# Moving the recurrence's right side and new state from VectorE to TensorE and ScalarE, in a delta-rule attention and mixture-of-experts kernel

## What is computed

```python
def step(S, inp):                                   # over the 2048 tokens
    q_t, k_t, v_t, b_t = inp
    v_new = (v_t - jnp.einsum('bhd,bhdm->bhm', k_t, S)) * b_t[..., None]
    S = S + jnp.einsum('bhd,bhm->bhdm', k_t, v_new)
    o_t = jnp.einsum('bhd,bhdm->bhm', q_t, S)
    return (S, o_t)
...
q = silu(_short_conv(x @ Wq.T, conv_q))             # the same for k and v; q, k normalized per head
...
final = (gathered * topk_w[:, :, None]).sum(1)      # 8 of 32 experts per token
```

## Time and profile before

| | |
|---|---|
| time, median of 3 runs | 3475.85 us (3452.18 to 3496.45) |
| the profiled execution | 3492.34 us, its span 3490.4 us |
| busy share of the span | PE 75%, DVE 62%, ACT 45%, POOL 30% |
| mean granted clock of PE | 0.853 |
| first phase | to about 1757 us |

### The profile page before, as it was taken

How to read it: one execution, slowest core, us unless ns; L and a number is a source line. 1 busy time by engine, 2 the same in 40 slices (tenths; PEclk the granted TensorE clock), 3 DMA queues, 4 the chain that set the end, 5 groups by cost and what they waited for, 6 DMA issues and landing times.

```text
span 3490.4 us, 109752 instructions
## 1 busy us (share of the span) xinstructions
PE 2631.6 (75%) x46188; PEld 1980.0 (57%) x46188; DVE 2150.8 (62%) x4702; ACT 1565.4 (45%) x2625; POOL 1051.2 (30%) x1028
## 2 busy tenths in 40 slices
PE   3568788887877888865389999978988898544354
PEld 2345555555555555554278888866777777322232
DVE  4779988888888988872332222123444444757665
ACT  4455554555555555511134444435545555323232
POOL 0000333233333333333321111044434431556560
PEclk8778888888888888866699999989999999776676
DMA  6000111111113311111189999977888886333331
GB/s 247 14 9 25 61 49 64 54 61 60 61 62 110 101 58 56 44 56 56 58 291 329 342 343 342 322 253 253 283 269 274 270 272 200 101 99 95 94 94 30
DMA packets 240349, 511.79 MB, mean 147 GB/s; under 512 B 38770, under 2 KB 63860, under 8 KB 239732
## 3 DMA queue, kind: packets, MB, share of 16 engines
q1 hardware_dynamic: 133396, 270.32, 23.5%
q0 software_dynamic: 49152, 134.28, 12.3%
q10 hardware_dynamic: 57312, 100.16, 7.9%
HBM read 303.82 MB, written 200.80 MB: 145 GB/s over the span
## 4 chain that ended last, share of the span: by engine, by line
DMA 53%; PE 25%; issue 7%; DVE 6%; ACT 4%; SPq 3%; POOL 0%; ACTq 0%; POOLq 0%; DVEq 0%
DMA scr_xs<-xn_r,idx 37%; DMA yg<-scr_ys,idx_y 15%; PE ps L632 11%; PE ps L640 6%; PE ps L621 3%; DVE tmp L1430 1%; DVE tu L1433 1%; SPq L823 1%; SPq L830 1%; DVE conv L1360 1%; PE ps L709 1%; DMA xt<-scr_xs 1%; PE ps L380 1%; PE ps L672 1%; DMA out<-x 1%
## 5 line engine op out<-in xcount | busy, mean ns | idle before, releaser
L855 POOL DMA_INDIRECT scr_xs<-xn_r,idx x512 | 531.1, 1037 | 1666.6 <-DMA scr_xs<-xn_r,idx 1325.4
L873 POOL DMA_INDIRECT yg<-scr_ys,idx_y x512 | 519.9, 1016 | 695.8 <-DMA yg<-scr_ys,idx_y 486.6
L632 PE MATMUL ps<-xT,wr 128*128 128x256 f32 x2544 | 616.4, 386 | 0.0
L1725 DVE TENSOR_TENSOR h<-sg,ps 128x256 f32<-128x256 f32 x318 | 133.1, 420 | 687.7 <-ACT sg L1110 687.3
L632 PEld LDWEIGHTS ps<-xT,wr 128*128 128x128 f32 x2544 | 469.9, 194 | 61.9 <-issue 8.6
L1752 DVE SCALAR_TENSOR_TENSOR x<-yg,wsel,x 128x256 f32<-128x256 f32 x512 | 248.0, 486 | 228.0 <-DMA yg<-scr_ys,idx_y 209.6
L640 PE MATMUL ps<-wr,h 128*128 128x256 f32 x1272 | 333.3, 385 | 60.3 <-DVE h L1725 34.2
L640 PEld LDWEIGHTS ps<-wr,h 128*128 128x128 f32 x1272 | 242.5, 192 | 100.8 <-DVE h L1725 36.6
L918 ACT ACTIVATE y<-ps 128x512 f32<-128x512 f32 x318 | 189.8, 597 | 204.2 <-PE ps L640 204.2
L1110 ACT ACTIVATE sg<-ps 128x256 f32<-128x256 f32 x318 | 122.0, 384 | 347.1 <-PE ps L632 346.3
L918 ACT ACTIVATE xT<-ps 128x512 f32<-128x512 f32 x382 | 225.4, 594 | 71.5 <-PE ps L621 36.2
(11 more groups left out here) (244 smaller groups left out, 4106.6 us busy)
## 6 DMA issues: line engine op xcount, KB each, us to landing
wr<-in_wexp SPq DMA_DIRECT2D x318, 384.0 KB, 4.9
xt<-scr_xs SPq DMA_DIRECT2D x318, 256.0 KB, 4.6
scr_ys<-y ACTq DMA_DIRECT2D x318, 256.0 KB, 4.5
scr_xs<-zeros SPq DMA_DIRECT2D x128, 256.0 KB, 3.1
x_in<-in_x SPq DMA_DIRECT2D x64, 128.0 KB
x_res<-in_x SPq DMA_DIRECT2D x64, 128.0 KB
scr_xs<-xn_r,idx POOLq DMA_INDIRECT x512, 3.2
scr_x<-x_res SPq DMA_DIRECT2D x16, 512.0 KB, 2.7
```

What stands on the lines that cost most here:

```text
L632: last = pe.matmul(ps[:, bank, half * TILE:(half + 1) * TILE], wr[:, t % NW, at:at + EI], xT2[:, t % NH, k, :], start=k == 0, stop=k == G - 1)
L855: nc.gpsimd.indirect_dma_start(xs[i // HB][:, :], bass.IndirectOffsetOnAxis(idx[:, i % NR, c, k:k + 1], 0), xn_r[:, i % NR, c, :], None).t ...
L873: nc.gpsimd.indirect_dma_start(yg[:, n % NG, k, :], None, ys[h][:, :], bass.IndirectOffsetOnAxis(idx_y[:, i, c, k:k + 1], 0))\
```

## The change

- `right_side` leaves DVE. A new function `from_inputs` on PE puts `bv` into the PSUM accumulator first (four matmuls of 32x32 by 256 columns per chunk, one for each quarter of the partitions, with the identity `eye` as weights), and `from_state` adds onto it. ACT then copies the sum to `r_sb`.
- `new_state` leaves DVE. ACT does it with two copies of 128 columns, each scaled by a column of `par`, which takes the place of the mask.
- DVE's last calls of a round were `solve_back`, `positions`, `products`, `new_inputs`, `shared_rows`, `token_rows`. They are now `solve_back`, `products`, `new_inputs`, `token_rows`, `shared_rows`, `positions`.
- The three lists of the round are laid anew. On PE the recurrence's calls follow each other sooner and `ranks` comes last. On ACT the calls are grouped so that fewer changes of the function table lie between them. The convolution goes in the order q, v, k instead of k, q, v.
- `token_rows` gets one more wait, for `from_state` of two blocks before. The second phase's code is not touched.

```diff
+            def from_inputs(j, c):
+                n = NC * j + c
+                pe.wait_ge(s_bv, j + 1)
+                if n:
+                    pe.wait_ge(s_rev, n)
+                    pe.wait_ge(s_uev, n)
+                for q in range(4):
+                    pe.matmul(ps[quad(q), RU, 0:D].rearrange("p (n m) -> p n m", m=2 * HD), eye[quad(q), :],
+                              bv[quad(q), j % 2, :, :, c, :].rearrange("p g b m -> p (g b) m"),
+                              start=True, stop=False, skip_group_check=True)
...
-                                                 s_sb[quad(q), g, b, :], start=kind == 0 or (g == 0 and b == 0),
-                                                 stop=kind == 0, skip_group_check=kind == 1)
+                                                 s_sb[quad(q), g, b, :], start=kind == 1 and g == 0 and b == 0,
+                                                 stop=kind == 0, skip_group_check=True)
...
-            CONV_ORDER = (2, 3, 0, 1, 4, 5)
+            CONV_ORDER = (0, 1, 4, 5, 2, 3)
...
+            def right_side(j, c):
+                n = NC * j + c
+                act.wait_ge(s_r, n + 1)
+                nc.scalar.activation(r_sb[:], ps[:, RU, 0:D], ACT.Copy).then_inc(s_rev, 1)
+
+            def new_state(j, c):
+                n = NC * j + c
+                act.wait_ge(s_ku, n + 1)
+                act.wait_ge(s_qs, n + 1)
+                for e in range(2):
+                    last = nc.scalar.activation(s_sb[:, :, :, e * HD:(e + 1) * HD].rearrange("p g b m -> p (g b) m"),
+                                                ps[:, ST, 0:D].rearrange("p (n e m) -> p n e m", e=2, m=HD)[:, :, e],
+                                                ACT.Copy, scale=par[:, e:e + 1])
+                last.then_inc(s_sev, 1)
...
-            def right_side(j, c):
-                n = NC * j + c
-                dve.wait_ge(s_r, n + 1)
-                dve.wait_ge(s_bv, j + 1)
...
-            def new_state(j, c):
-                n = NC * j + c
-                dve.wait_ge(s_ku, n + 1)
-                dve.wait_ge(s_qs, n + 1)
...
                 if Bs:
                     solve(26, 31)
+                if Ps:
+                    gated(p, 1)
+                if Bs:
                     solve_back(b_)
-                if Ps:
+                if A:
+                    products(a)
+                    new_inputs(a)
+                    token_rows(a)
+                if Ps:
+                    shared_rows(p)
                     positions(p)
-                if A:
-                    products(a)
```

More of the change, by code:

```diff
@@ L584, in _ @@
                     project(a, 6)
+                if Ps:
+                    logits(p)
                 if C:
                     to_state(j, 2)
+                if Ps:
+                    shared_up(p, "SU", 1, 0)
+                    shared_up(p, "SG", 0, 1)
+                if C:
                     to_output(j, 2)
                 if A:
+                    norms(a, 1)
+                if C:
+                    from_inputs(j, 3)
+                if A:
                     norms(a, 0)
+                    norms(a, 3)
                 if C:
@@ L1032, in _ @@
                     key_halves(b_)
+                if C:
+                    right_side(j, 0)
+                    new_values(j, 0)
                 if Ps:
@@ L1082, in _ @@
                     betas(a, 0)
+                if Ps:
+                    sigmoids(p)
+                if A:
+                    silus(a, 2)
+                    silus(a, 3)
+                if C:
+                    new_state(j, 2)
+                if Ps:
+                    gate(p, 1)
                 if C:
@@ L1092, in _ @@
                 if C:
-                    new_values(j, 3)
-                if A:
-                    raised(a, 2)
-                    norms(a)
-                    silus(a, 5)
-                if C:
+                    right_side(j, 3)
+                if A:
+                    raised(a, 0)
+                    raised(a, 2)
+                    silus(a, 5)
+                    norms(a)
+                if C:
+                    new_values(j, 3)
                     new_rows(j, 3)
+                    new_state(j, 3)
             def tile_in(t):
@@ L1652, in _ @@
                     solve(7, 11)
-                if C:
-                    right_side(j, 1)
-                if Bs:
                     solve(11, 14)
-                if A:
-                    taps(a, 2, 3)
-                if Bs:
-                    solve(14, 16)
-                if C:
-                    new_state(j, 1)
-                if Bs:
-                    solve(16, 19)
-                if Ps:
-                    gated(p, 0)
                 if A:
@@ L1669, in _ @@
                 if Bs:
+                    solve(14, 16)
+                    solve(16, 19)
+                if A:
+                    taps(a, 4, 5)
+                if Bs:
                     solve(19, 22)
-                if C:
-                    right_side(j, 2)
+                if A:
+                    taps(a, 2, 3)
+                if Ps:
+                    gated(p, 0)
                 if Bs:
```

168 lines of the change are left out of this document (70 added, 98 removed).

## The result

| | before | after |
|---|---|---|
| median of 20 runs each, same sessions | 3476.03 us (3452.18 to 3496.45) | 3494.95 us (3472.31 to 3508.68) |
| ratio, 95% interval | | 1.0049 (1.0029 to 1.0069) |
| the profiled execution, its span | 3492.34, 3490.4 us | 3500.18, 3498.4 us |

The change is 0.5% slower. That is far within the 2% of which I spoke, but its interval is clear of 1, and on the other side than the forecast of 3466 us. It lies inside the range of 3425 to 3500 us.

What follows compares the result with a forecast made beforehand. The string of one-at-a-time scatters was taken to bound the first phase; start -2.6, pace -9 and tail +2 us made about -10 us, so 3475.85 became 3466 us, range 3425 to 3500 us.

Steps and rivals of the forecast that it cites:

- The frame: First phase's end: start 326.4 us, plus 13 blocks of scatters (1397.3 us), plus 34.7 us of tail; round length not in it.
- The string: POOL's unbroken run of 512 scatters from `xn_r`, each waiting for the one before; 108.7 us a block against 96.2 a round.
- the crossing: Block from which `route_rows` waits for scatters of three blocks earlier; forecast at p = 9.2, so block 10 instead of 13.
- The start: First scatter, after `positions` of block 0: 5.1 and 6 us gained, 8.5 lost, -2.6 us in all (-7 to +6).
- The tail: Last `route_rows` to first tile load: `choose` 4 us earlier, `positions` behind `shared_down` 6 us later, +2 us (0 to +5).
- The pace: Time per scatter over 416 scatters: more standing time in shorter rounds speeds them, -9 us (0 to 18 gained).
- The rounds: One `route_rows` to the next: 96.2 to about 92 us (88 to 99), from DVE savings and fewer waits, less 1 us on PE.
- The upper bound: PE's sixteen new small matmuls a round priced as full ones of 386 ns: 6.2 us, against the 1.0 taken.
- the second rival: PE becomes the bound, slowed by waits on ACT; decides only from 101.9 us a round; 3515 us at 105; chance 0.06.
- standing rounds: Rounds of blocks 10 to 13, each with some 13 us more standing time, 53 us in all, letting scatters run faster.
- The first: Rival: rounds don't get shorter, as waits for ACT replace those for DVE; 3475 us; chance 0.16.
- The third: Rival: scatters quicken and the rounds' gain comes through; 3349 us, or 3410 at 3.2 us a scatter; chance 0.10.

Runs made afterwards that it cites:

- a_early: Kernel after with `positions` before `products` and `ranks` before `shared_down` again, in all rounds; ratio to the kernel before 1.0010.
- a_early0: Kernel after with `positions` and `ranks` moved forward again only in the round of block 0; ratio to the kernel before 1.0024.
- a_early15: Kernel after with `positions` and `ranks` moved forward again only in the last round, block 15; ratio to the kernel before 1.0031.
- b_late: Kernel before with `positions` moved to the end of DVE's round; ratio to the kernel before 1.0039.
- b_math: Kernel before with the change's arithmetic alone (`from_inputs` on PE, `right_side` and `new_state` on ACT), other calls in the old order; ratio 1.0040.
- b_k1: Kernel before with one of eight scatters left and the second phase's tiles read from a zeroed stretch; ratio to the kernel before 0.9752.
- aeg_f11: Kernel after with `positions` and `ranks` early, second `gated` early, two scatters in flight from block 11; ratio to the kernel before 1.0231, chip 5.
- b_flight2b: Kernel before with two scatters in flight throughout, on chip 10; ratio to the kernel before 0.9816.
- b_f11: Kernel before with two scatters in flight from block 11 on, on chip 7; ratio to the kernel before 0.9831.
- b_f11b: Kernel before with two scatters in flight from block 11 on, on chip 5; ratio to the kernel before 1.0173.
- b_f11c: Kernel before with two scatters in flight from block 11 on, on chip 10; ratio to the kernel before 0.9809.

## Why the prediction was wrong, point by point

**The frame held.** The string is unbroken, its start, its pace and the tail set the end of the first phase, and a round isn't in the sum as long as it stays below the crossing. a_early, a_early0, a_early15 and b_late move start and tail and with them the time; b_math makes the rounds 5 us longer and they still don't enter the sum; b_k1 gives the 1645 us that the rounds reach alone. This is so on chips like 7 and 10; on 5 and 9 rounds and string are near a tie.

The forecast failed in the terms. The start was to gain 11.1 us against a cost of 8.5, and gained 3.4 against a cost of 11.1. The tail was to gain 4 us from an earlier `choose`, which was no earlier, and its detour cost 7.4 instead of 6. The pace was to give 9 us from shorter rounds, which got longer, and gave 1.6.

**The start: +7.8 us instead of -2.6, outside of its bounds (-7 to +6).** The cost was right as far as it went (8.5 us for the calls that `positions` was moved behind), but a wait that the move makes was missing, and the gain was too large. The timeline of DVE of the kernel after, in round 1:

```profile
317.83 1.18 DVE L1426 SCALAR_TENSOR_TENSOR nq<-conv,sq 128x1024 f32<-128x1024 f32 x1
...
327.54 1.28 DVE L1609 TENSOR_TENSOR x_res<-x_res,ps 128x512 f32<-128x512 f32 x2 [2.61 <-PE ps L512]
```

`products` starts at 317.83 us. Before, `positions` stood at the same place in the list, behind `solve_back`. It started at 321.18 us:

```profile
321.18 0.25 DVE L1552 TENSOR_TENSOR posv<-ps,ecap 128x128 f32<-128x128 f32 x1
```

So rounds -2 to 1 gained 3.4 us, not the 11.1 that I had added up (5.1 for the removed operations and 6 for the waits behind them). The operations are gone, but DVE came to its next wait for PE sooner by as much: `products` of round 0 did start 7.3 us earlier (224.2 against 231.5 us), and in round 1 the waits of `pair_tiles` for PE (5.69, 1.01 and 3.81 us before the first three) gave most of it back. Behind `products` DVE waits 2.61 us for `shared_down`, a call that `positions` had not stood behind. Then 8.5 + 2.6 - 3.4 = 7.7, near the 7.8 of the scatter.

And even the 3.4 us are within the spread. The three kernels with the new arithmetic and `positions` in its early place (a_early, a_early0, aeg_f11) start the string at 321.3, 325.9 and 327.6 us, and the ten with the old arithmetic and the early place at 320.9 to 327.4.

**The tail: +7.4 us instead of +2 (bounds 0 and +5).** The timeline of DVE in the last round of the kernel after:

```profile
1752.62 0.68 DVE L1602 TENSOR_TENSOR h_s<-sq_o,ps 128x512 f32<-128x512 f32 x1
1760.24 1.29 DVE L1609 TENSOR_TENSOR x_res<-x_res,ps 128x512 f32<-128x512 f32 x2 [6.94 <-PE ps L512]
```

I had `choose` 4 us earlier for its new place between the two `gated`. It ends 23.5 us after `route_rows` in both kernels. Then the second `gated`, behind it, lets `shared_down` start only then, and DVE, with nothing else to do, waits 6.94 us for it before `positions`. The sixteen records of `shared_down` take 6.73 us here against 4.60 before; the granted clock over them is 0.54, near the lower of its two levels (1.2 GHz), and was 0.78. PE had stood idle for 4.68 us before them. Before the change `shared_down` ran beside `positions`, and nothing in the tail waited for it. I had counted 6 us for the detour and a gain that did not exist.

**The rounds: 98.1 us instead of 92 (bounds 88 to 99).** Two sizes were off. DVE's own saving was 2.45 us a round, near the 2.7 to 3.3. PE's cost was not 1.0 us. The groups by line of PE in ten rounds of the kernel after (count, busy us, mean ns):

```profile
L392 PE MATMUL ps<-bv,eye 32*32 32x256 f32 x320 | 31.8, 460 | 1.4 <-issue 1.4
```

That is 3.2 us a round. I had the price of a column from the earlier trace rows, where "128 small matmuls" stand in 1.99 us. The trace has two records for each float32 matmul: these 16 matmuls a round show as 32 records, and so the 128 records of the earlier trace rows were 64 matmuls. By that the same sum gives 2.0 us; the rest of the miss is that wide 32x32 matmuls run less densely than the narrow ones. The upper bound was halved in the same way: the 2544 records of the earlier trace rows are 4 matmuls for each of 318 tiles, so that a full matmul has two records of 386 ns and sixteen make 12.4 us. With that in place of 6.2, a round could have passed the 101.9 us of the second rival, and its condition was not as far away as I wrote. And the waits moved instead of ending: 4.2 us a round that stood on `r_sb` and `s_sb` no longer do (1.3 more stand as "issue" before `solved`), those for `h_s` rose from 2.6 to 4.9 us. PE's account of a round is 78.8 busy, 9.0 issue, 8.3 waits for DVE and ACT before, and 80.9, 10.4 and 6.5 after.

**The pace: -1.6 us instead of -9.** This term hung on the rounds. It needed four more standing rounds; with longer rounds the waits fell from 73.8 to 55.0 us instead of growing to 110 to 140, and there was less rest in which a scatter could run faster. (By the prediction's own numbers the crossing comes at p = 9.1 and not 9.2; that changes nothing.) Over the first 320 scatters the pace even rose, from 3.395 to 3.428 us, and the last 96 before the tail gave it back. So taking eight DVE operations a round away, which read PSUM, did not quicken the string. The Trainium skill, SBUF — State Buffer (SBUF: two separate sides), says that GpSimd can't write its descriptors while a DVE operation of a two-port mode holds the pair of ports that they share. The pace does not speak against it, but no run here separates these operations from such ones.

**The rivals.** The first, that the rounds don't get shorter, was the right one, and it had given 3475 us. Of the other 20 us to the measured 3495, the two terms above, that stood in its sum as well, are 15.8 us in the profiled pair; the rest stays open (below). The second was half right: PE is the engine that grew. It didn't decide, because 98.1 us is below the 101.9 that it needed; b_math, at 101.4 with 2.2 us of waits left, shows that the 101.9 were about right. The third has its answer in b_flight2b and b_f11: the string can be quickened, and it then gives what it promised up to the rounds (first tile at 1692 and 1689 us), on some chips.

**What stays open.** The profiled pair is 7.8 us apart, the medians 19 us. The profiled execution of before lies 16.3 us above its median (3492.3, median 3476.0), that of after 5.2 us (3500.2, median 3494.9), so some 11 us of the difference lie in how far one execution stands from its median. I suppose that they lie in its pace, since 0.03 us on 416 scatters is 12 us, but no profile of a median execution of before is there to show it. b_late and a_early bear out 13 of the 19 us for the place of `positions`, each with an interval of some 8 us either way; for the last 5 us, which are within the intervals, I have no cause. The 5.6 us that the second phase gave back in the profiled pair are within its spread: from the first tile to the end it takes 1722 to 1733 us in three traces of the same program (b_f11, b_f11b, b_f11c).

## What to carry to other kernels

Where one string of transfers paces a phase, work taken off the busiest engine bought nothing here: look first for what starts the string and for what stands behind it at its end, and don't move the call that does either behind something that isn't needed for it. When a call is moved, list the waits of the calls that it is now behind, and not their durations alone. When operations are taken from an engine that waits for its partner a few calls later, count the saving up to that wait, not for the whole round.

## What the runs showed of the hardware

- Two indirect scatters in flight raise the throughput from 32 in 108 us to 32 in 54 to 62 us on one chip and 32 in 46 to 53 us on another, and PE pays for it on the second alone: its "issue" time at the small matmuls of L380 is 137.9 us in ten rounds on one chip and 31.8 us on another, with the same program; the whole kernel goes to 1.0964 and to 0.9816. A kernel tuned with this on one chip can lose on the next: the gain or loss went with the chip in all four that were tried, each in one session.
- Chips differ with one scatter in flight too: the kernel before takes 3459 to 3469 us on two of them and 3478 to 3485 us on two others. The same program (b_f11) has 3.29 us a scatter on chip 5 and 3.38 and 3.39 on chips 7 and 10. In ten rounds PE is busy there for 835 us and for 790 and 793 us with the same matmuls, at a mean granted clock of 0.84 and 0.85. So a chip with faster scatters had slower rounds.
- A float32 matmul stands in the trace as two records (320 for the 160 of L392 in ten rounds, 2544 for the 1272 of L632). Four 32x32 matmuls of 256 columns, side by side in the four quarters, take 0.8 us (31.8 us for 40 of these groups).
